# A hybrid transformer block on one core: spreading ScalarE's softplus steps over units, and a new order of TensorE's last matmuls

## The reference

```python
x = x + attn_block(layernorm(x))    # x: 8 x 512 x 128, float32
x = x + ffn(layernorm(x))           # quantised W, plus a low-rank term, plus bias
# attn_block(x), with xn = layernorm(x) * ln_g + ln_b:
delta = softplus(dt_in @ w_dt + b_dt)                    # dt_in, B, C = xn @ w_xproj
h = exp(delta * A) * h + (delta * xn) * B;  y = h @ C    # scan over 512 steps, 128 x 64 states
ssm_out = (y + x * D_ssm) @ w_ssm_out
attn_out = local_attention(x) @ wo       # 16 heads, blocks of 32, window of three blocks
conv_out = silu(conv4(x) + b_conv)
mem_out = x @ w_wm + b_wm + 0.3 * softmax(x @ dec.T / sqrt(128)) @ dec
return x + 0.2 * attn_out + 0.45 * ssm_out + 0.15 * conv_out + 0.2 * mem_out
```

## Time and profile before

| | us |
|---|---|
| median of 3 runs | 1116.49 (1115.62 to 1121.41) |
| the profiled execution: its own time | 1114.23 |
| its span, first to last instruction | 1112.4 |
| mean granted clock of TensorE | 0.871 of full |

### The profile page before, as it was taken

How to read it: one execution, slowest core, us unless ns; L and a number is a source line. 1 busy time by engine, 2 the same in 40 slices (tenths; PEclk the granted TensorE clock), 3 DMA queues, 4 the chain that set the end, 5 groups by cost and what they waited for, 6 DMA issues and landing times. The chain is left out here.

```text
span 1112.4 us, 19145 instructions
## 1 busy us (share of the span) xinstructions
PE 830.9 (75%) x4151; PEld 339.3 (30%) x4151; DVE 979.3 (88%) x2299; ACT 837.5 (75%) x2255; POOL 955.6 (86%) x675
## 2 busy tenths in 40 slices
PE   5367878688777786877778777867868778677775
PEld 2023333233323332333323333323332333232332
DVE  2688999979997999979999699897999799999991
ACT  4468886788778878687877887679887887858871
POOL 6369988989898988988899898899989898979892
PEclk9556998978997989979898798888899798989897
DMA  5845667647675666666676476665666566766630
GB/s 111 196 126 169 180 159 185 171 138 198 163 183 155 185 167 159 172 157 172 168 203 161 128 191 162 167 173 159 177 176 183 153 187 165 188 161 164 196 95 9
DMA packets 124391, 181.18 MB, mean 163 GB/s; under 512 B 29263, under 2 KB 41056, under 8 KB 124256
## 3 DMA queue, kind: packets, MB, share of 16 engines
q1 hardware_dynamic: 123968, 179.56, 61.4%
q10 hardware_dynamic: 288, 0.20, 0.1%
HBM read 170.79 MB, written 5.05 MB: 158 GB/s over the span
## 5 line engine op out<-in xcount | busy, mean ns | idle before, releaser
L1389 POOL TENSOR_TENSOR prod<-hst,C 128x1024 f32<-128x1024 f32 x256 | 602.0, 2354 | 94.9 <-DVE hst L1201 94.4
L1201 DVE TENSOR_TENSOR_SCAN hst<-decay,bank 128x512 f32<-128x512 f32 x384 | 459.5, 1209 | 3.0 <-DVE cv_a L1236 2.8
L1189 DVE TENSOR_TENSOR bank<-bank,B 128x512 f32<-128x512 f32 x384 | 263.1, 685 | 52.6 <-PE bank L911 34.8
L665 ACT ACTIVATE decay<-wide,A_rep 128x512 f32<-128x512 f32 x384 | 273.4, 715 | 41.5 <-DVE hst L1201 31.2
L911 PE MATMUL bank<-spread,sel_bc 96*128 96x512 bf16 x384 | 164.5, 434 | 101.0 <-DVE hst L1201 90.6
L679 ACT ACTIVATE prob<-s_sb,nmax 128x96 f32<-128x96 f32 x512 | 185.2, 365 | 0.9 <-DVE nmax L1214 0.5
L1405 POOL TENSOR_TENSOR uwide<-uwide,B 128x512 f32<-128x512 f32 x128 | 162.7, 1271 | 22.5 <-DMA uwide<-u_rows 22.5
L935 PE MATMUL bank<-prod,sel_red 128*32 128x512 f32 x1024 | 164.9, 722 | 0.0
L1201 DVE TENSOR_TENSOR_SCAN hst<-bank,uwide 128x512 f32<-128x512 f32 x128 | 155.4, 1214 | 2.7 <-POOL uwide L1405 2.7
L951 PE MATMUL bank<-ident,prob 128*96 128x128 f32 x512 | 85.9, 295 | 77.5 <-ACT ao L695 58.3
L944 PE MATMUL bank<-k,q 128*128 128x384 f32 x256 | 126.7, 580 | 22.3 <-DVE nmax L1214 22.2
(11 more groups left out here) (189 smaller groups left out, 1027.4 us busy)
## 6 DMA issues: line engine op xcount, KB each, us to landing
wide<-dt_rows SPq DMA_DIRECT2D x512, 256.0 KB, 4.7
uwide<-u_rows SPq DMA_DIRECT2D x128, 256.0 KB, 4.1
spread<-parts SPq DMA_DIRECT2D x66, 32.0 KB, 4.1
x_sb<-in_L_attn_x_dram SPq DMA_DIRECT2D x8, 256.0 KB, 4.5
dt_rows<-sp_t SPq DMA_DIRECT2D x8, 256.0 KB, 2.6
out_dram<-outb SPq DMA_DIRECT2D x8, 256.0 KB, 3.9
vw<-v_tok SPq DMA_DIRECT2D x80, 16.0 KB, 3.3
u_rows<-uv SPq DMA_DIRECT2D x8, 64.0 KB, 2.4
```

The lines of the kernel that those rows point to most:

```text
L665: nc.scalar.activation(to, wide[m % SLOTS][:, s % 2, :], ACT.Exp, scale=A_rep[:, g:g + 1]).then_inc(exp_done, 1)
L1189: v.tensor_tensor(uP[s % 4][:, :], uP[s % 4][:, :], B2[p][:, :], ALU.mult).then_inc(dbx_done, 1)
L1201: v.tensor_tensor_scan(hst[:, s % 8, :], kept, into[:, :], 0.0, ALU.mult, ALU.add).then_inc(scan_done, 1)
L1389: g.tensor_tensor(prod[:, 2 * (m % 4):2 * (m % 4) + 2, :], hst[:, 2 * (m % 4):2 * (m % 4) + 2, :], C2[p][:, :].unsqueeze(1).to_broadcast([ ...
```

## The change

The softplus is spread. Exp stays at unit 20; +1 becomes `softplus_sum` at 21, -1 becomes `softplus_less` at 22, and Ln moves from 21 to 25. All that follows moves by four units: the four GpSimd steps to 26 to 29, `high` to 32, `r` to 34, `mid` to 37, `lo` to 39, and SyncE's stores of the rows and of the parts by two pairs of units. In the last body the projection steps are dealt out otherwise (n = 0 to 5 at units 60 and 61, none at 62), in the tail the last reduction goes ahead of the steps 8 and 9, and the bias matmul goes into the free bank `sP`, between the transposes ahead of the norm and those behind it; the small matmul and the output of the last sequence use that bank.

```diff
-LAST_PROJECT = {60: (0, 1), 61: (2, 3), 62: (4, 5), 63: (6, 7)}
+LAST_PROJECT = {60: (0, 1, 2), 61: (3, 4, 5), 63: (6, 7)}
...
-    "ln_stats": 0, "ln_aggr": 2, "ln_root": 4, "ln_apply": 11, "scale_xn": 12, "softplus_exp": 20,
-    "softplus_logs": 21, "lost": 22, "log1p": 23, "dt": 24, "u": 25, "high": 28, "r": 30,
-    "mid": 33, "lo": 35,
+    "ln_stats": 0, "ln_aggr": 2, "ln_root": 4, "ln_apply": 11, "scale_xn": 12, "softplus_exp": 20, "sum": 21, "less": 22,
+    "softplus_logs": 25, "lost": 26, "log1p": 27, "dt": 28, "u": 29, "high": 32, "r": 34,
+    "mid": 37, "lo": 39,
...
-ROWS_AT = {"store": 15, "rows": 14}
+ROWS_AT = {"store": 15, "rows": 16}
-PART_DMA_AT = {16: 0, 18: 1, 20: 2}
+PART_DMA_AT = {18: 0, 20: 1, 22: 2}
...
                 nc.scalar.activation(sp_e[:, :], sp_e[:, :], ACT.Exp, scale=-1.0).then_inc(sp_step, 1)
+
+            def softplus_sum(B):
                 wait(act, sp_step, B * N_SP + SP["exp"])
                 nc.scalar.activation(sp_t[:, :], sp_e[:, :], ACT.Identity, bias=1.0).then_inc(sp_step, 1)
+
+            def softplus_less(B):
                 wait(act, sp_step, B * N_SP + SP["sum"])
...
-            def ffn_half(h):
+            def ffn_half(h, job=jobP):
...
+                ffn_bias(jobP)
+                ffn_half(0)
+
+            def ffn_bias(job):
+                mm(job[:, :], ones_row[:, :], bias_row[:, :].unsqueeze(1).to_broadcast([1, NT, D]), start=True, stop=False,
                    skip_group_check=True)
-                ffn_half(0)
...
             def tail(B, p):
+                reduce_group(B, GROUPS - 1)
                 for n in range(8, N_PROJ - 1):
                     project(B, p, n)
-                reduce_group(B, GROUPS - 1)
                 project(B, p, N_PROJ - 1)
                 tail_job("back", B, p)
+                wait(pe, s_max, NB * NBLK)
+                ffn_bias(sP)
                 tail_job("zT", B, p)
-                ffn_begin(B)
-                tail_job("ffn", B, p)
+                wait(pe, done["t"], job_count("t", B, "zT"))
+                ffn_half(0, sP)
+                filled(ffn_half(1, sP), "t", B, "ffn")
```

More of the change, by code:

```diff
@@ L642, in front @@
                         softplus_exp(B)
+                        softplus_sum(B)
+                        softplus_less(B)
                         softplus_logs(B)
@@ L796, in body @@
                             softplus_exp(B + 1)
+                        if s == AT["sum"]:
+                            softplus_sum(B + 1)
+                        if s == AT["less"]:
+                            softplus_less(B + 1)
                         if s == AT["softplus_logs"]:
@@ L1004, in project @@
                     filled(ins, "t", B, "proj")
-            def ffn_half(h):
+            def ffn_half(h, job=jobP):
                 for t in (2 * h, 2 * h + 1):
-                    ins = mm(jobP[:, t * D:(t + 1) * D], zT[:, t * 128:(t + 1) * 128], W2[:, :], start=False, stop=True,
+                    ins = mm(job[:, t * D:(t + 1) * D], zT[:, t * 128:(t + 1) * 128], W2[:, :], start=False, stop=True,
                              skip_group_check=True)
@@ L1014, in ffn_begin @@
                 fill("t", B, "ffn")
-                mm(jobP[:, :], ones_row[:, :], bias_row[:, :].unsqueeze(1).to_broadcast([1, NT, D]), start=True, stop=False,
+                ffn_bias(jobP)
+                ffn_half(0)
+            def ffn_bias(job):
+                mm(job[:, :], ones_row[:, :], bias_row[:, :].unsqueeze(1).to_broadcast([1, NT, D]), start=True, stop=False,
                    skip_group_check=True)
-                ffn_half(0)
             def tail_job(name, B, p):
@@ L1260, in output @@
                 wait_job(dve, "t", B, "ffn")
-                v.tensor_tensor(outb[:, :, :], jobP[:, :].rearrange("p (t d) -> p t d", t=NT), x1[:, :, :], ALU.add) \
+                v.tensor_tensor(outb[:, :, :], (sP if last(B) else jobP)[:, :].rearrange("p (t d) -> p t d", t=NT), x1[:, :, :], ALU.add) \
                     .then_inc(out_ready, 1)
```

## The result

| | before | after |
|---|---|---|
| median of 15 runs, us | 1116.49 (1112.78 to 1126.86) | 1124.25 (1118.82 to 1131.58) |
| profiled execution: its time, span | 1114.23, 1112.4 | 1120.36, 1118.6 |
| mean granted clock of TensorE | 0.871 | 0.861 |

The ratio is 1.0068, 95% interval 1.0045 to 1.0092: the changed kernel is 0.7% slower. The forecast was 0.5% faster, with a range that ends at 1121.

The account below looks back on a forecast made before the run. VectorE, busy 979 of 1112 us, was taken to bound the kernel, with GpSimd (956) right behind. Bodies 7.2 gained, less 4.5 for TensorE's clock, plus 2.6 in the tail: 5.3 us gained, 1111 us, range 1094 to 1121.

Parts of the forecast that it names:

- The second wait: VectorE at the inverse of the softmax sums, unit 24: falls from 3.5 to about 0.1 us once Ln's block moves.
- The first wait: VectorE ahead of unit 24's multiply, 2.59 us in body 3, from the copy of block 9's output: not touched by the change.
- scores of block 24: TensorE's scores, needed by unit 26's multiply, are late next; they end at 491.6 in body 3 and that end stays.
- decay of unit 28: Ln's block in unit 25 makes this ScalarE step late for VectorE: an estimated 0.5 us.
- The chain of 16.0 us: GpSimd's gapless work from scan 25's end through `u`; holds `high`, `mem_exp`, `mem_inv`, leaving 7.2 us gained over seven bodies.
- Unit 38: VectorE waits for scores after TensorE idles ahead of the B projection: 0.65 us a body, 4.5 in all, bounds 0 and 28.
- The 28 us that I had hung on the rule: Sum over seven bodies if, by the skill page's clock rule, new idle time costs each a slow restart; the half-clock end.
- The later steps: `r`, `mid`, `lo` in their new units are the same work under the same load: 0, bounds 0 and 0.5 us a body.
- SyncE at 0: SyncE's moved stores hold only `widen` for units 42 and on, wanted six units later: 0 us.
- The tail: End of the kernel: 0.7 us from the last reduction going earlier, 1.9 from the moved bias matmul; 2.6 us gained.
- Slower: Rival: TensorE's clock falls ahead of each B projection, half until unit 36's scores; up to 28 us, 1134; chance 0.17.
- The gain stays: Rival: GpSimd finishes `u` before ScalarE reaches `high`; 21 us, with the tail 24, giving 1093; chance 0.2.

Follow-up runs that it names:

- the tail alone: Changed kernel with the softplus steps and SyncE's places as before, so only the tail is new: 1112.57 us, ratio 0.9969 to the kernel before.
- the two half changes: Two kernels, each with half the change: only the new tail, ratio 0.9969; only the spread and shifted softplus with the old tail, 1128.93 us, ratio 1.0113.
- The filler: Changed kernel plus five zero-weight matmuls on TensorE just ahead of the B projection: 1112.17 us, ratio 0.9958; the same in the kernel before: 1135.07 us, 1.0166.
- short steps: Changed kernel with `lost`, `log1p`, `dt` and `u` done on 16 of 512 columns from the second sequence on: 1104.86 us, ratio 0.9895.

## Why the prediction was wrong, step by step

- **The second wait.** Forecast to fall from 3.5 to about 0.1 us: it is 0 in body 3, and 0.3 in all. Right, and it was Ln's block, as the kernel with +1 and -1 back at 20 shows.
- **The first wait untouched; scores of block 24 next; decay of unit 28 late.** 2.59, 0.97 and 0.79 us in body 3, against 2.59, some 0.8 and 0.5. Right.
- **The chain of 16.0 us and `mem_inv`.** 16.04 us measured, ScalarE's wait for `u` 2.57 in place of 3.3 (2.5 to 3.7 in the seven bodies), `mem_inv`'s wait 2.01. The sum up to M, -7.05, meets the -7.2 forecast more closely than two executions can tell: the last tenths are luck. 1.81 of it lies in body 0, where 0.1 was forecast, but the tail alone, whose bodies are those of the kernel before, also reaches M 1.29 earlier there. Bodies 1 to 6 gave 5.2 in this pair and 7.3 in the pair of the two half changes, for 7.1. Mechanism and size hold within 2 us. What the prediction had not seen is that `u` isn't the only item: the normalisation at the same place in GpSimd's queue holds `mem_inv` by another way when `u` is moved.
- **Unit 38: the step that failed first, by its size.** "I take 0.65, since [...] most of the 4.7 us came at full clock again in body 5". Measured: 0.87 to 1.73 us in each of seven bodies, 8.9 in all instead of 4.5. The half-clock bound of 4.0 was far off too. The stretch of 4.7 us took 6.8 (515.05 to 521.88), where the term of 0.65 allows 6.05 (5.4 and 0.65) and the bound of 4.0 has 9.4. The clock fell in all seven bodies; before, in two. The filler shows that clock and wait belong together, in five bodies of seven. The Trainium skill, TensorE: Matmul & The Clock Gate (What's actually happening), calls half clock the state of rest. By that rule each idle stretch costs a slow restart. The trace of the changed kernel agrees with it in seven bodies of seven. With +1 and -1 back at 20 the projection of body 6 took only 1.32 us behind 3.35 us of idle time, and half clock came with the reduction behind it. The 28 us that I had hung on the rule are not borne out, since full clock was back ahead of unit 36's scores.
- **The later steps: the step that failed outright.** "`mid` in unit 37 (0.6 us) [...] find ScalarE and GpSimd with the load they had in units 33 and 35 [...]: 0, with bounds of 0 and 0.5". Measured: 0.86 us a body, 6.0 in all. `mid` takes 0.62 us of ScalarE ahead of the `ao_copy` for which the next transposes wait, with the taps of the convolution right behind these, and VectorE wants the gate at a fixed distance from M. Moving `mid` by one unit takes 3.6 of the 6.0 away; the other 2.4 are open. I had asked who needs `mid`, and not who stands behind it.
- **Behind `mem_inv`.** A scan waits 0.25 us in six bodies, 1.5 in all, with `issue` as its releaser; what lies behind it the trace doesn't say. Not forecast. With 8.9 and 6.0 this makes 16.4 of the 17.4 us beyond M. The rest is bookkeeping: the recorded lines of VectorE cover 15.20 instead of 14.96 us of this stretch in each body, 1.7 in all (probably the small overlap of neighbours, which is lost at each stop), less the 0.65 that the gate had waited in all before.
- **SyncE at 0.** Right as far as the list of waits shows: no new wait of VectorE for a transfer came up.
- **The tail.** 3.1 us for 2.6: 1.1 up to the norm instead of 0.7, and 2.0 behind it, for 1.9. The tail alone has a ratio of 0.9969.
- **The sum.** -5.3 forecast, +6.1 measured, 11.4 apart: 4.4 at unit 38, 6.0 at the gate, 1.5 at the scan, 1.0 more in M to C, less 1.15 between C and S and 0.5 in the tail, and 0.15 the other way up to M. By the median the forecast was 1111, and 1124.25 came.
- **The rivals.** "Slower" had the right mechanism, and its price of a slow restart, 1.27 us a body, is just short of the 1.4 from which it was to decide; together with `mid` and the scan, 2.5 us a body (17.4 / 7), it passes the 2.2 that it needed. One mechanism alone would not have done it. "The gain stays" is what the kernel with steps two units apart comes near to: 22.4 us up to M, for 24.5 + 6 - 9 = 21.5 there, though 6.4 come back beyond M and the time is 18 us below the kernel before, not 24. Its condition, that GpSimd be done with `u` before ScalarE comes to `high`, is needed but not enough: `u` in unit 28 met it in seven bodies and won nothing. What the spacing adds is that the normalisation of block 24 comes earlier and `high` no longer stands ahead of `mem_exp`; which of the two does more, no run tells.

## What to carry to other kernels

A block of work that is moved off one engine's critical place drags its successors along: lay out the queue of each engine that serves them from the last point where it was idle, and ask of each moved step not only who needs it but who stands behind it. Here the engine with 85% load had idle places just ahead of the moved steps and none among them; spacing the steps by two units, with `high` behind `mem_exp`, gave three times the gain up to that point. A step that is late is not always the only late one at its place: moving one of two only shows the other. Where a wait opens on TensorE, count a slow restart with it, and look for the slack at the place it restarts.

## What the hardware showed that I had not expected

- The same place came at either clock. Ahead of the B projection, 3.0 to 3.6 us idle gave half clock in seven bodies of seven (changed kernel), 1.5 us in five of six (short steps; body 0 had 1.93 us and kept full clock), 0.19 us in two of seven (kernel before) and in three of seven (the tail alone, the same bodies). So the length of the last idle time doesn't tell the clock by itself.
- Matmuls whose product is not used hold the clock: 4.48 us of them gave a B projection of 1.13 instead of 2.08 us. Where no idle time was there to fill, the same five took 4.48 us in three bodies and about 6 in four, and made the kernel 1.7% slower.
- The moved block of two table loads and Ln has no gap here either (ScalarE of the changed kernel), so its 3.2 us (496.67 to 499.89) are all that it costs ScalarE; the next decay starts at 499.90:

```profile
496.67 1.28 ACT L626 ACT_TABLE_LOAD   x1
497.96 0.63 ACT L626 ACTIVATE sp_l<-xn 128x512 f32<-128x512 f32 x1
498.61 1.28 ACT L671 ACT_TABLE_LOAD   x1
```
